# Ranking wide rows: a second coupling of each row's larger halves, and a new table of beats

## What is computed

```python
q, k = l2norm(q), l2norm(k)                      # 16 heads of 64, 4 memory keys ahead of the 256
dots = jnp.einsum('bhid,bhjd->bhij', q, k) * QK_SCALE
dots = jnp.einsum('hg,bgij->bhij', W_pre_th, dots)      # heads mixed
dots = jnp.where(causal[None, None], mask_value, dots)
top = jax.lax.top_k(dots, TOPK)[0]                      # TOPK = 64
vk = top[..., -1:]
dots = jnp.where(dots < vk, mask_value, dots)
attn = jax.nn.softmax(dots, axis=-1)
attn = jnp.einsum('hg,bgij->bhij', W_post_th, attn)     # heads mixed again
out = jnp.einsum('bhij,bhjd->bhid', attn, v) * head_scale_params
out = out.transpose(0, 2, 1, 3).reshape(b, n, H * DH) * jax.nn.sigmoid(x @ Wg + bg)
return out @ Wo
```

## Time and profile before

| what | value |
|---|---|
| three runs | 4073.38, 4079.89, 4090.41 us; median 4079.89 |
| the profiled execution | 4078.01 us, its span 4076.7 us |
| mixer, then the change-over | to about 1000 us |
| attention | about 1000 to 4077 us: 32 rankings, about 94 us a period |
| busy over the span | PE 89%, DVE 90%, ACT 78%, POOL 18% |
| mean granted TensorE clock | 0.964 of full |

### The profile page before, as it was taken

One profiled execution on the slowest core, in us unless ns is written; L12 is line 12 of the kernel. 1 busy time (PEld: TensorE's weight loads), 2 busy tenths in 40 slices (PEclk: granted clock), 3 DMA queues, 4 the chain that ended last, 5 costly groups with the idle time before them and its releaser, 6 DMA issues. The chain is left out here.

```text
span 4076.7 us, 78506 instructions
## 1 busy us (share of the span) xinstructions
PE 3616.2 (89%) x19551; PEld 2619.3 (64%) x19551; DVE 3666.3 (90%) x19933; ACT 3190.1 (78%) x10112; POOL 750.4 (18%) x2495
## 2 busy tenths in 40 slices
PE   3999999975799899999999999989999999999987
PEld 2888888862566666666666666666666666666655
DVE  6888888841999999999999999999999999999995
ACT  4677777746788888888888888888888888888863
POOL 2000000010222222222222222222222222222221
PEclk7999999986899999999999999999999999999998
DMA  3000000001111111111111111111111111111110
GB/s 118 7 11 12 13 11 11 9 10 30 25 26 26 26 29 29 26 27 33 33 30 26 27 26 26 26 27 30 27 26 27 31 31 32 27 26 27 25 25 4
DMA packets 168120, 105.97 MB, mean 26 GB/s; under 512 B 78000, under 2 KB 165104, under 8 KB 166896
## 3 DMA queue, kind: packets, MB, share of 16 engines
q1 hardware_dynamic: 167664, 100.96, 11.8%
HBM read 20.70 MB, written 8.91 MB: 7 GB/s over the span
## 5 line engine op out<-in xcount | busy, mean ns | idle before, releaser
L1544 DVE MAX8 last<-W 128x8 f32<-128x130 f32 (+17 forms) x4032 | 942.5, 274 | 0.0
L1526 DVE MATCH_REPLACE8 W<-last,W 128x130 f32<-128x130 f32 (+17 forms) x3456 | 871.9, 259 | 0.0
L650 DVE TENSOR_TENSOR_SCAN hs<-dA,dx 128x256 f32<-128x256 f32 x512 | 349.5, 683 | 127.0 <-issue 99.4
L1640 POOL TENSOR_SCALAR posts<-post,share 128x128 f32<-128x128 f32 x1024 | 368.9, 380 | 514.8 <-DVE share L1458 512.1
L1083 PE MATMUL bank<-T,pre 128*128 128x40 f32 (+15 forms) x1024 | 368.7, 443 | 72.5 <-DMA T<-SN 48.0
L1313 ACT ACTIVATE SN<-bank,rq 128x260 f32<-128x260 f32 (+1 forms) x1024 | 361.3, 431 | 88.1 <-PE bank L1070 73.8
L1093 PE MATMUL bank<-posts,T 128*128 128x128 f32 (+7 forms) x2048 | 386.8, 292 | 3.2 <-POOL posts L1640 2.7
L1070 PE MATMUL bank<-kT,qT 64*128 64x260 f32 (+1 forms) x2048 | 274.1, 371 | 116.4 <-ACT SN L1313 110.5
L1093 PEld LDWEIGHTS bank<-posts,T 128*128 128x128 f32 (+7 forms) x2048 | 281.0, 170 | 93.8 <-issue 55.8
L1083 PEld LDWEIGHTS bank<-T,pre 128*128 128x128 f32 x1024 | 168.5, 195 | 216.4 <-ACT T L1319 95.4
L1253 ACT ACTIVATE E<-T,peak 128x260 f32<-128x260 f32 (+12 forms) x800 | 305.3, 432 | 2.7
(11 more groups left out here) (238 smaller groups left out, 8843.6 us busy)
## 6 DMA issues: line engine op xcount, KB each, us to landing
T<-SN SPq DMA_DIRECT2D x32, 130.0 KB
x_in<-in_xT SPq DMA_DIRECT2D x32, 128.0 KB, 2.3
x_mid<-x_b SPq DMA_DIRECT2D x32, 128.0 KB, 1.7
xb<-x_mid SPq DMA_DIRECT2D x32, 128.0 KB, 2.1
out_y<-x_d SPq DMA_DIRECT2D x32, 128.0 KB, 3.4
T<-SN SPq DMA_DIRECT2D x32, 126.0 KB
T<-SN SPq DMA_DIRECT2D x32, 122.0 KB
T<-SN SPq DMA_DIRECT2D x32, 118.0 KB
```

The costliest lines, as they stand in the source:

```text
L650: dve.tensor_tensor_scan(hs[j % NH][:], dA[j % ND][:], dx[b % 2][:], 0.0, ALU.mult, ALU.add).then_inc(scanned, 1)
L1526: dve.match_replace(both[:, s, at:to], best[n], both[:, s, at:to], LOWEST).then_inc(ranked, 1)
L1544: dve.max(best[n], both[:, s, at:to]).then_inc(ranked, 1)
L1640: pool.tensor_scalar(posts[(4 * k + j) % NP][:], post[:], share[k % 2][:, j:j + 1], 1.0, ALU.mult, ALU.mult).then_inc(posts_made, 1)
```

## The change

`wide` gets a second coupling. The larger ones of the couples (h elements) are now written to `W[h:w]`, and their left and right halves are coupled once more, with q = w/4: the larger into `W[0:q]`, the smaller into `W[q:h]`. So two more TENSOR_TENSOR on 2 x q elements per pair, the first of which waits for the first coupling. The first two rounds then work on q elements (MAX8 of `top` and of the first `done`, MATCH_REPLACE8 of `done` 0 and 1); from the third round on all is as before, on `W[0:h]`. `rank_steps` counts 19 steps for a wide group where it counted 18. Number and sizes of all other ranking instructions stay.

With it most entries of the table of beats are changed. Of these only those that the prediction speaks of are shown:

```diff
@@ rank_steps
-        n = sum(18 for g in QUAD[i] if g in WIDE) + (QUAD[i][2] not in WIDE)
+        n = sum(19 for g in QUAD[i] if g in WIDE) + (QUAD[i][2] not in WIDE)
@@ the table of beats
-    DVE_SHARE = (36, 38, 50, 65, 89, 98, 120, 130)
-    DVE_GATES = (19, 21, 25, 27)
+    DVE_SHARE = (27, 37, 60, 64, 93, 96, 119, 129)
+    DVE_GATES = (19, 20, 24, 26)
     DVE_END1 = 61
-    DVE_GATED = (77, 77)
+    DVE_GATED = (78, 78)
@@ wide
-            w, h = width(g), width(g) // 2
+            w, h, q = width(g), width(g) // 2, width(g) // 4
...
-            dve.tensor_tensor(both[:, :, 0:h], x[:, :, 0:h], x[:, :, h:w], ALU.max).then_inc(ranked, 1)
+            dve.tensor_tensor(both[:, :, h:w], x[:, :, 0:h], x[:, :, h:w], ALU.max).then_inc(ranked, 1)
             paired = count = count + 1
             yield
             dve.tensor_tensor(both[:, :, w:w + h], x[:, :, 0:h], x[:, :, h:w], ALU.min).then_inc(ranked, 1)
+            count += 1
+            yield
+            dve.wait_ge(ranked, paired)
+            dve.tensor_tensor(both[:, :, 0:q], both[:, :, h:h + q], both[:, :, h + q:w], ALU.max).then_inc(ranked, 1)
+            paired = count = count + 1
+            yield
+            dve.tensor_tensor(both[:, :, q:h], both[:, :, h:h + q], both[:, :, h + q:w], ALU.min).then_inc(ranked, 1)
...
-                dve.max(best[n], both[:, s, 0:h]).then_inc(topped if j == 3 else ranked, 1)
+                dve.max(best[n], both[:, s, 0:q]).then_inc(topped if j == 3 else ranked, 1)
...
-                at, to = ((0, h), (h, w), (h, h + w))[(done >= 4) + (done >= 6)]
+                at, to = ((0, q), (0, h), (h, w), (h, h + w))[(done >= 2) + (done >= 4) + (done >= 6)]
...
-                at, to = ((0, h), (h, w), (h, h + w))[(done >= 3) + (done >= 5)]
+                at, to = ((0, q), (0, h), (h, w), (h, h + w))[(done >= 1) + (done >= 3) + (done >= 5)]
```

More of the change, by code:

```diff
@@ L867, in cuts @@
         return CUTS_ALL * b + sum(len(c) for c in CUTS[:i]) + sum(x <= j for x in CUTS[i])
[L870 to L877, removed]
+    PE_K = (-18, -16, 5, 6)
+    PE_K_TURN = (8, 23, 24, 26)
+    PE_Q = (25, 27, 29, 41)
+    PE_Q_SUM = (32, 37, 45, 47)
+    PE_Q_TURN = 48
+    PE_ATTEND = (10, 13, 18, 19)
@@ L878, in attention_phase @@
+    PE_GATES = (46, 47, 48, 51)
+    PE_MIX = (41, 53, 55, 91, 114, 120, 129, 132)
     PE_MIX_STEP = 0
[L879 to L882, removed]
+    PE_OUT = 23
+    PE_VAR1 = 31
+    PE_SPREAD1 = 50
+    PE_W1 = 53
     PE_W2 = 57
[L884 to L888, removed]
-    PE_VAR2 = 106
-    PE_SPREAD2 = 111
-    PE_V = (115, 118, 125, 132)
-    PE_PREMIX = [[72, 87, 90, 95, 102, 109, 113, 118], [121, 128, 129, 131, 132, 137, 152, 156]]
@@ L893, in attention_phase @@
[L893 to L896, removed]
-    ACT_Q_SUM = 50
[L898 to L904, removed]
+    PE_H1 = (62, 65, 66, 68)
+    PE_H2 = (69, 72, 73, 79)
+    PE_SCORE0 = (54, 56, 57)
+    PE_W3 = 86
@@ new lines, in attention_phase @@
+    PE_SCORE1 = (80, 86, 88, 95, 97, 99, 103, 104)
+    PE_VAR2 = 106
+    PE_SPREAD2 = 112
+    PE_V = (114, 116, 124, 133)
+    PE_PREMIX = [[72, 87, 90, 95, 102, 107, 113, 118], [121, 128, 129, 131, 132, 137, 152, 156]]
+    ACT_K = (-25, -19, 0, 0)
+    ACT_K_TURN = (4, 24, 28, 34)
+    ACT_Q = (34, 37, 45, 46)
+    ACT_K_ROOT = (-11, 7)
+    ACT_Q_SUM = 50
+    ACT_Q_ROOT = 56
+    ACT_PEAK = (-1, 2, 34, 48, 64, 70, 81, 103)
+    ACT_WIDE = (-1, 19, 37, 50, 65, 73, 85, 103)
+    ACT_NARROW = (2, 30, 40, 50, 67, 73, 87, 113)
@@ L905, in attention_phase @@
+    ACT_MIX = (47, 54, 73, 100, 104, 111, 120, 126)
+    ACT_SQUARE1 = 36
+    ACT_ROOT1 = 40
     ACT_SET = (41, 52, 68, 79)
-    ACT_GATES = (47, 48, 50, 51)
-    ACT_SILU = (60, 61)
+    ACT_GATES = (48, 49, 51, 52)
+    ACT_SILU = (60, 64)
     ACT_SCORE0 = (64, 66, 67)
[L909 to L915, removed]
@@ L916, in attention_phase @@
-    DVE_SHARE = (36, 38, 50, 65, 89, 98, 120, 130)
-    DVE_GATES = (19, 21, 25, 27)
+    ACT_H1 = (68, 70)
+    ACT_H2 = (76, 78)
+    ACT_SCORE1 = (79, 81, 85, 89, 90, 90, 91, 93)
+    ACT_SQUARE2 = 88
+    ACT_ROOT2 = 93
+    ACT_V = (106, 112, 117, 126)
+    ACT_PREMIX = [[75, 84, 86, 89, 90, 99, 104, 108], [110, 116, 118, 120, 125, 148, 157, 166]]
+    DVE_SHARE = (27, 37, 60, 64, 93, 96, 119, 129)
+    DVE_GATES = (19, 20, 24, 26)
     DVE_END1 = 61
-    DVE_Q_CLIP = 61
-    DVE_GATED = (77, 77)
+    DVE_Q_CLIP = 60
@@ L921, in attention_phase @@
+    DVE_GATED = (78, 78)
     DVE_END2 = 117
[L922 to L930, removed]
+    POOL_TURN = (-88, -37, -36, 2, 18, 45, 56, 57)
+    POOL_SHARE = (5, 6, 30, 42, 56, 73, 94, 113)
+    POOL_ROOT1 = 13
@@ L932, in whose @@
+    POOL_Q_ROOT = 30
+    POOL_ROOT2 = 57
+    POOL_PREMIX = [[68, 69, 73, 74, 76, 77, 90, 90], [101, 106, 125, 126, 133, 145, 150, 165]]
+    ACT_K_SCALE = (-7, 27)
+    POOL_K_CLIP = (-43, -9)
+    POOL_K_ROOT = (-20, -9)
     def whose(p, t, beat, lag=1):
```

## The result

The changed kernel takes 4113.98 us (median of 4 runs, 4106.17 to 4124.56), the kernel before 4080.98 us beside it. The ratio is 1.0081, with a 95% interval of 1.006 to 1.0102: slower by about 33 us, where 32 were forecast. The profiled execution of the changed kernel took 4117.35 us, its span is 4116.0.

The account below looks back on a forecast made before the run. A ring without slack was taken as the bound: DVE from second gate to `f_a`, then PE, ACT and DMAs to the next gate. +0.85 and +0.22 us over 30 periods add 32 to 4078.0: 4110 us, range 4060 to 4126.

Parts of the forecast that it names:

- DVE's part of the ring: DVE's stretch from second gate to the `f_a` products, on the path: 36.65 us growing by 0.85 to 37.50 a period.
- the three pairs of slots 2 to 4: Wide pairs ranked between second gate and `f_a`: the coupling was to save 0.11, 0.08 and 0.07 us.
- The coupling's share of it: On DVE: shorter MAX8 and MATCH_REPLACE8 save 3.74 us, added TENSOR_TENSOR cost 2.9 to 3.1; 0.65 us lighter a sequence.
- the wait ahead of the third TENSOR_TENSOR costs nothing: In each wide pair on DVE: the second one's 0.2 us or more cover the first's 0.28 us duration; cost zero.
- Rival 1: DVE's whole work sets the end, gate waits being soft: 21 us less, 4058 us; chance 0.15.
- PE's part: Stretch from `f_a` to the next second gate, 57.66 us: mean from `f_a` to `f_b` up 0.22 us a period.
- The slow hidden layers 1: On PE, 8.86 us instead of 7.17, at granted clock 0.50: expected 27 of 32 where there were 18.
- Its bounds, none slow and all slow: Limits for PE from `f_a` to `f_b`: -1.1 us a period with no slow hidden layer 1, +0.45 with all slow.
- rival 2: Ring holds, clock falls no more often or less: 4098 us, or 4073 with no slow hidden layer; chance 0.25.
- What would show it: Signs: gate to `f_a` 37.5 us, gate waits and `f_a` wait each 60 or more, DVE below 97%.
- Rival 3: ACT's freed 2.56 us and earlier `E` shorten scores to attend; at 2 us a period 4050 or less; chance 0.06.
- Rival 4: Durations count on DVE: added TENSOR_TENSOR cost 4.4 us against 3.74 saved, ring +1.5 a period, 4125 us; chance 0.04.

Follow-up runs that it names:

- c_gated77: The changed kernel with the two `f_a` products at beat 77 instead of 78: 4064.51 us, ratio 0.9946.
- k_order75: The ranking of the kernel before (one coupling) with all new beats, but the `f_a` products at beat 75: 4022.71 us, ratio 0.9849.
- f_gated75: The changed kernel with the two `f_a` products at beat 75 instead of 78: 4013.54 us, ratio 0.9819.
- b_order: The ranking of the kernel before (one coupling) with all new beats of the changed kernel: 4123.57 us, ratio 1.0091.
- a_coupling: The changed kernel's ranking (second coupling) with all beats of the kernel before: 4089.24 us, ratio 1.0006.
- d_filled: The changed kernel plus two unread PE matmuls ahead of hidden layer 1 in each period: 4072.58 us, ratio 0.9966.
- g_added_slot2: The changed kernel plus one unread MAX8 on 740 elements in slot 2, between second gate and `f_a`: 4117.85 us, ratio 1.0068.

## Why the prediction was right

**DVE's part of the ring**: forecast +0.85, to 37.50 us. Measured +0.96 in the mean and 37.52 to 37.53 in most periods. The two large terms were read off the order and came as forecast: the MAX8 on 122 that moved behind the second gate take 0.38 us, those on 196 ahead of `f_a` 0.54, and `c_gated77` gives the latter back. The rest is errors that cancel. The moved MATCH_REPLACE8 brought 0.09 where 0.19 was forecast, a score product on 228 took 0.11 less, which no term had, and the three pairs of slots 2 to 4 took 0.05 more where the coupling was to take 0.26 off.

**The coupling's share of it was too large.** The sum took 0.65 us a sequence for DVE's lighter work, and "the wait ahead of the third TENSOR_TENSOR costs nothing". Counted from start to next start with idle time left out, DVE got 0.34 us lighter from `k_order75` to `f_gated75` and 0.43 from `b_order` to the changed kernel, but 0.10 heavier from before to `a_coupling`. The second holds for the third itself, but the fourth holds DVE longer than its elements in several pairs. In the ring this was 0.26 us of terms, none of which came; they were small beside the order's. Rival 1, the saving seen in full at 4058, fell on both counts: the ring, and a saving of at most two thirds of the size.

**PE's part**: forecast +0.22 (27 of 32 slow, `f_b`'s wait gone). Measured +0.02. The wait for `f_b` went, as the prediction said, and is worth what it said: a period without a fall of the clock needs 7.74 us from `f_a` to `f_b` where 7.9 was worked out. The slow hidden layers 1 were 23, and 4 of these took 10.2 us, a kind that the prediction did not have; it expected 27, and its 18 for the kernel before were 17. Its bounds, none slow and all slow, bracket the effect: `d_filled` has one slow and needs 1.28 us a period less from `f_a` to `f_b` than the changed kernel. In size this part lies midway between the forecast and rival 2, by which it was to fall by 0.22: the falls came more often, yet cost less than worked out.

**What would show it**: the wait for `f_a` grew to 57.1 us (60 or more was expected), DVE's busy share fell to 96.2% (below 97%), `f_b`'s wait went. The gates' wait reached 44.4 us and not 60: the rest of DVE's idle time came at `x_d`, 56.9 us, since DVE gets there early for the same PE. Gates and `x_d` together rose by 43 us. The wait for `E` did not shrink (40.5 and 40.6 us); that step was wrong, and nothing hung on it, as the prediction said.

**Rival 2**, no more falls of the clock, would have given 4098; the falls did come more often, 23 against 17. Rival 3, a gain through ACT's order, did not show: to the mix on 512 and from there to the gate nothing got shorter. Rival 4 said that the added instructions cost their durations. They take 3.54 us where durations give 4.4 and starts 2.77, so the truth lies between. The Trainium skill (VectorE: DVE Perf Modes, The DRAIN you can't avoid), by which the next op waits for an empty pipe, disagrees with the trace of the changed kernel too: L1513 starts 0.16 us after L1510, whose duration is 0.25. The same section adds that a next op that is not held starts earlier, which the prediction left out; the trace agrees with that sentence. And 4125 would have needed the ring to carry it, and most added ones stand outside. The period grew by 1.23 us where 1.07 was forecast. That the total is so near, 33 us against 32 and 4114 against 4110, owes something to errors that cancel: DVE's part 0.1 above, PE's 0.2 below, the stretch ahead of the mix on 512 0.15 above.

## What to carry to other kernels

When two engines hand work to and fro, the cost of an instruction is decided by its place: the same MAX8 cost 23 us between the wait and the hand-over and nothing behind it. Before an engine's work is made lighter, look where it last waits and what it does from there until it releases the other; here one number in a table, which moved two products three beats forward, brought 100 us, and the lighter ranking 9. Then move by steps and time each, since three beats further on the products met their own input.

## What the hardware showed beyond that

A wait of some 1.7 us on PE costs twice. In the changed kernel the 57.1 us of waiting for `f_a` brought 41 us of slower matmuls, and PE's two unread matmuls of 1.88 us in the gap took them away. Whether the clock falls is not told by the wait alone: 1.66, 1.68 and 1.71 us were followed by a granted clock of 1.00, 0.50, and 0.50 for longer, and a kernel with more waiting (`g_added_slot2`, 58.5 us) had fewer falls. In the kernel before, 30 hidden layers 1 stood behind waits of 1.23 to 1.26 us; 17 took 8.8 us or more, 13 took 7.2.

On DVE neighbouring instructions overlap by about 0.1 us, but not always: a TENSOR_TENSOR of 0.25 us held the engine 0.16 us when another TENSOR_TENSOR followed and 0.22 us when a MAX8 on its predecessor's result did. A shorter one before such a MAX8 held it 0.14 us, so the dependence alone does not explain it.
